# Self attention in four column tiles, and engine loops written out, in a small diffusion transformer

## The reference, cut to what matters

```python
h = (1 + scale_a) * layernorm(x) + shift_a
q, k, v = split(h @ W_qkv + b_qkv, 3)          # 16 heads of 8 features
o = softmax(q @ k.T / sqrt(8)) @ v             # self attention, 56 x 56 for each head
x = x + gate_a * (o @ W_proj + b_proj)
...
x = x + attention(layernorm(x) @ W_q, ctx @ W_kv) @ W_cproj   # 1500 context rows
x = x + gate_m * mlp((1 + scale_m) * layernorm(x) + shift_m)
```

## Time and profile before

| | us |
|---|---|
| median of 3 runs | 1056.95 (1056.18 to 1058.56) |
| the profiled execution | 1058.8 |
| its span, first to last instruction | 1057.0 |
| TensorE busy | 920.5 (87%) |
| VectorE busy | 575.2 (54%) |
| ScalarE busy | 509.2 (48%) |
| GpSimd busy | 362.3 (34%) |

### The profile page before, as it was taken

How to read it: one execution, slowest core, us unless ns; L and a number is a source line. 1 busy time by engine, 2 the same in 40 slices (tenths; PEclk the granted TensorE clock), 3 DMA queues, 4 the chain that set the end, 5 groups by cost and what they waited for, 6 DMA issues and landing times.

```text
span 1057.0 us, 24684 instructions
## 1 busy us (share of the span) xinstructions
PE 920.5 (87%) x9363; PEld 595.3 (56%) x9363; DVE 575.2 (54%) x1265; ACT 509.2 (48%) x754; POOL 362.3 (34%) x481
## 2 busy tenths in 40 slices
PE   5758999999787897978999999988698899999977
PEld 3435666666554444943666666654494466666653
DVE  7566566667232564135666666615313666666725
ACT  5555666665412114212666666531413366666541
POOL 6654555561000115046655554010312333333000
PEclk9688999999999996666999999999858799999999
DMA  9752443337327204316334333110413544443200
GB/s 261 174 146 60 118 119 103 106 88 244 120 75 205 59 0 124 84 39 160 102 105 111 106 110 88 27 59 1 126 43 95 132 118 118 117 116 88 61 1 9
DMA packets 76824, 106.27 MB, mean 101 GB/s; under 512 B 9370, under 2 KB 70426, under 8 KB 76480
## 3 DMA queue, kind: packets, MB, share of 16 engines
q1 hardware_dynamic: 75152, 102.26, 34.9%
q10 hardware_dynamic: 1584, 2.79, 0.9%
HBM read 41.17 MB, written 0.23 MB: 39 GB/s over the span
## 4 chain that ended last, share of the span: by engine, by line
PE 58%; DVE 15%; issue 14%; ACT 6%; POOL 3%; DMA 2%; SPq 1%; ACTq 0%; POOLq 0%; DVEq 0%
PE oacc_ps L579 10%; PE ring_ps L553 9%; PE score_ps L567 7%; PE ring_ps L537 6%; DVE max_sb L686 6%; PE ring_ps L530 6%; PE oacc_ps L895 4%; PE ring_ps L1173 3%; PE oacc_ps L334 2%; PE ring_ps L543 2%; PE ring_ps L522 2%; ACT key_sb L641 1%; POOL hat_sb L755 1%; DMA prob_sb<-ctx_T 1%; DMA nat_sb<-ctx_nat 1%
## 5 line engine op out<-in xcount | busy, mean ns | idle before, releaser
L686 DVE TENSOR_REDUCE max_sb<-ring_ps 128x1 f32<-128x500 f32 x576 | 356.3, 672 | 175.8 <-PE ring_ps L553 175.8
L659 ACT ACTIVATE prob_sb<-score_ps 125x896 f32<-125x896 f32 x288 | 257.2, 919 | 133.1 <-PE score_ps L567 132.2
L553 PE MATMUL ring_ps<-kstack,qstack 128*128 128x500 bf16 x576 | 204.4, 393 | 24.7 <-DVE max_sb L686 16.8
L764 POOL TENSOR_TENSOR key_sb<-key_sb,part_sb 128x500 f32<-128x500 f32 x72 | 81.9, 1137 | 282.8 <-ACT key_sb L641 282.8
L567 PEld LDWEIGHTS score_ps<-qstack,kstack 128*128 128x128 bf16 (+1 forms) x2304 | 145.4, 102 | 48.8 <-issue 8.1
L567 PE MATMUL score_ps<-qstack,kstack 128*128 128x112 bf16 (+3 forms) x2304 | 167.5, 214 | 2.5 <-ACT qstack L663 2.3
L579 PE MATMUL oacc_ps<-prob_sb,val_sb 125*32 125x168 f32 (+1 forms) x3456 | 140.2, 295 | 12.7 <-ACT prob_sb L659 12.3
L579 PEld LDWEIGHTS oacc_ps<-prob_sb,val_sb 125*32 125x32 f32 x3456 | 98.1, 110 | 51.9 <-ACT prob_sb L659 23.6
L553 PEld LDWEIGHTS ring_ps<-kstack,qstack 128*128 128x128 bf16 (+1 forms) x576 | 52.6, 98 | 111.1 <-issue 59.8
L755 POOL TENSOR_SCALAR hat_sb<-nat_sb,norm_now 125x128 f32<-125x128 f32 x192 | 87.6, 471 | 5.0 <-POOL norm_now L745 5.0
L771 POOL TENSOR_TENSOR part_sb<-key_sb,part_sb 128x500 bf16<-128x500 f32 x72 | 81.7, 1134 | 5.8
(11 more groups left out here) (208 smaller groups left out, 1038.0 us busy)
## 6 DMA issues: line engine op xcount, KB each, us to landing
kstack<-part_sb SPq DMA_DIRECT2D x432, 125.0 KB, 2.4
nat_sb<-ctx_nat SPq DMA_DIRECT2D x22, 672.0 KB
nat_sb<-ctx_T SPq DMA_DIRECT2D x8, 750.0 KB, 4.4
qstack<-qpart_sb SPq DMA_DIRECT2D x24, 224.0 KB, 3.6
w_sb<-ctx_nat SPq DMA_DIRECT2D x5, 672.0 KB
w_sb<-weights SPq DMA_DIRECT2D x1, 3076.5 KB, 12.7
prob_sb<-ctx_T SPq DMA_DIRECT2D x4, 750.0 KB, 7.3
tok<-ctx_nat SPq DMA_DIRECT2D x3, 672.0 KB
```

The costliest lines, as they stand in the source:

```text
L553: last = pe.matmul(ps[:, 0:KB], queries(p, n, D), kstack[:, u, p, j * KB:(j + 1) * KB], start=True, stop=True)
L659: ins = act.activation(dst, score_ps[0:CK, c % 2, :, 0:HALF], ACT.Exp)
L686: ins = dve.tensor_reduce(max_sb[:, p, j:j + 1], ring_ps[:, self.bank[name], 0:KB], AX.X, ALU.max)
L764: ins = pool.tensor_tensor(rest, rest, part_sb[:, 0, cols], ALU.subtract)
```

## The change

What it does:

- Self attention: the values are the weights now (56 x 32, of which the first 8 columns belong to the head), the probabilities move (56 columns). The four heads 4a to 4a+3 go to four column tiles, so a batch is 4 x 4 matmuls, and the result stands feature by token, with heads on partitions 0, 32, 64, 96 of four rows `a`. Four more matmuls with weights of ones and 4 x 56 moving columns give the sums. Two PSUM banks take turns. VectorE takes the reciprocal of 128 x 224 sums and multiplies 128 x 224 results, batch by batch; transposes and the bias step are gone.
- The bias of v is added by two matmuls in the stage that makes the values.
- The projection takes four products for each pair of batches, with weights that are spread over 4 x 128 rows with zeros between, and the first three pairs run in the stage.
- All engine loops are written out, and addresses and counts are constants. `settle` is removed wherever it stood.

```diff
-def later_periods(body, eng, after_first=None):
+def later_periods(body, after_first=None):
...
-    with eng.Fori(0, (B - 4) // 2) as j:
-        body((2 * j, 0, j), (2 * j + 1, 1, j), (2 * j + 2, 0, j + 1), (2 * j + 3, 1, j + 1))
-        body((2 * j + 1, 1, j), (2 * j + 2, 0, j + 1), (2 * j + 3, 1, j + 1), (2 * j + 4, 0, j + 2))
+    for n in range(B - 4):
+        body(*((k, k % 2, k // 2) for k in range(n, n + 4)))
...
-        own_val = sb("own_val", [LQ, B, NH, OW])
+        own_val = sb("own_val", [LQ, B * D + GW])
...
+        own_o = tok[:, 7:11, :]
...
-        def settle(eng):
-
-            eng.sem_inc(settled, 1)
...
+                self.banks = [oacc_ps[:, :], ring_ps[:, 1, :]]
+
+            def outputs(self, n, part):
+
+                cols = OWN_ROWS * LQ
+                return self.banks[n % 2][:, part * cols:(part + 1) * cols].rearrange("p (a q) -> p a q", q=LQ)
...
                 for b in range(B):
                     last = pe.matmul(score_ps[0:LQ, 0, b // 4, (b % 4) * D:(b % 4 + 1) * D], by_batch(xh_t)[:, b, :],
-                                     self.wval, start=True, stop=True)
+                                     self.wval, start=(b % 4 == 0), stop=False, skip_group_check=True)
+                for i in range(2):
+                    last = pe.matmul(score_ps[0:LQ, 0, i, :].rearrange("p (b k) -> p b k", b=4),
+                                     self.bval.broadcast_to([D, LQ]),
+                                     ident[:, :].unsqueeze(1).broadcast_to([D, 4, D]), start=False, stop=True,
+                                     skip_group_check=True)
...
-                def pair(i, more):
-                    pe.wait_ge(s["normed"], i + 1)
-                    for r in range(2):
-                        pe.wait_ge(s["probs"], 2 * i + r + 1)
-                        for h in range(NH):
-                            last = pe.matmul(oacc_ps[0:LQ, (r * NH + h) * OW:(r * NH + h + 1) * OW],
-                                             prob_sb[0:LQ, r, h * LQ:(h + 1) * LQ], own_val[:, 2 * i + r, h, :],
-                                             start=True, stop=True)
-                        last.then_inc(s["attended"], 1)
...
+                def attend(n):
+
+                    r = n % 2
+                    if n >= 2:
+                        pe.wait_ge(s["finished"], n - 1)
+                    pe.wait_ge(s["probs"], n + 1)
+                    probs = prob_sb[0:LQ, r, :].rearrange("p (a t q) -> p a t q", t=4, q=LQ)
+                    for a in range(OWN_ROWS):
+                        for t in range(4):
+                            at = n * D + (4 * a + t) * HD
+                            pe.matmul(self.outputs(n, 0)[t * GW:(t + 1) * GW, a, :], own_val[:, at:at + GW],
+                                      probs[:, a, t, :], start=True, stop=True, skip_group_check=True)
+                    for t in range(4):
+                        last = pe.matmul(self.outputs(n, 1)[t * GW:(t + 1) * GW, :, :], own_val[:, B * D:B * D + GW],
+                                         probs[:, :, t, :], start=True, stop=True, skip_group_check=True)
+                    last.then_inc(s["attended"], 1)
...
+                for n in range(B):
+                    attend(n)
+                    if n + 2 < B:
+                        scores(n + 2, n % 2)
+                    if n >= 3 and n % 2:
+                        pe.wait_ge(s["finished"], n - 1)
+                        project(pe, (n - 3) // 2)
+                pe.wait_ge(s["finished"], B)
+                project(pe, B // 2 - 1)
...
+                for n in range(B):
+                    act.wait_ge(s["scores"], n + 1)
+                    if n >= 2:
+                        act.wait_ge(s["attended"], n - 1)
+                    act.activation(prob_sb[0:LQ, n % 2, :].rearrange("p (h q) -> p h q", h=2),
+                                   score_ps[0:LQ, n % 2, :, 0:HALF], ACT.Exp).then_inc(s["probs"], 1)
...
+                sums = T(6)[:, 0:OWN_ROWS * LQ].rearrange("p (a q) -> p a q", q=LQ)
+                for n in range(B):
+                    dve.wait_ge(s["attended"], n + 1)
+                    if n:
+                        dve.wait_ge(s["finished"], n)
+                    dve.reciprocal(sums, self.outputs(n, 1)).then_inc(s["sums"], 1)
+                    dve.wait_ge(s["sums"], n + 1)
+                    dve.tensor_tensor(own_o[:, :, n * LQ:(n + 1) * LQ], self.outputs(n, 0), sums, ALU.mult)\
+                        .then_inc(s["finished"], 1)
...
+        def project(l):
+
+            def product(pe, i):
+                cols = slice(2 * i * LQ, 2 * (i + 1) * LQ)
+                for a in range(OWN_ROWS):
+                    last = pe.matmul(d_mid[l].ps("proj")[:, cols], w(NAMES[l]["proj"], a), own_o[:, a, cols],
+                                     start=(a == 0), stop=(a == OWN_ROWS - 1))
+                if i == B // 2 - 1:
+                    d_mid[l].pe.done(last, "proj")
+            return product
...
-                keep_busy(pe, 2)
-                pe.wait_ge(*last_output(att_own[l]))
-                d.product(pe, "proj", [(w(nm["proj"]), o_t)])
```

More of the change, by code:

```diff
@@ L33 @@
 FIRST_ROW = 2
-OW = HD + 1
+OWN_ROWS = 4
 GW = 32
@@ L796, in later @@
                 emit = self.emitter(eng)(engine)
-                later_periods(lambda *batches: self.run(eng, engine, emit, *batches), engine, after_first)
+                later_periods(lambda *batches: self.run(eng, engine, emit, *batches), after_first)
             def load_nat(self, sp, n, u):
@@ L833, in sync_later @@
                 self.sync_batch(sp, (0, 0, 0), (1, 1, 0))
-                with sp.Fori(0, (B - 4) // 2) as j:
-                    self.sync_batch(sp, (2 * j + 1, 1, j), (2 * j + 2, 0, j + 1))
-                    self.sync_batch(sp, (2 * j + 2, 0, j + 1), (2 * j + 3, 1, j + 1))
+                for n in range(1, B - 3):
+                    self.sync_batch(sp, (n, n % 2, n // 2), (n + 1, (n + 1) % 2, (n + 1) // 2))
                 self.sync_batch(sp, (B - 3, 1, B // 2 - 2), (B - 2, 0, B // 2 - 1))
@@ L914, in tensor @@
                     scores(r, r)
-                for i in range(B // 2):
-                    pair(i, i < B // 2 - 1)
+                for n in range(B):
[7 more added lines that the diff above has]
+                project(pe, B // 2 - 1)
             def scalar(self, act, meanwhile):
@@ L1823 @@
         a[name] = a[name][..., cols]
+    for name in ("L2_W_proj", "L3_sa_proj_w"):
+        rows = np.zeros((OWN_ROWS, 4, GW, D), np.float32)
+        rows[:, :, 0:HD, :] = a[name].reshape(OWN_ROWS, 4, HD, D)
+        a[name] = rows
     blocks = [a[name].reshape(n, D, cols).transpose(1, 0, 2).reshape(D, n * cols) for name, n, cols in WEIGHTS]
```

62 lines of the change are left out of this document (7 added, 55 removed), and 4 rows, old and new, of the table WEIGHTS.

## The result

The changed kernel takes 1018.05 us (median of 1014.28, 1017.0, 1019.09 and 1021.3), the kernel before 1056.97 beside it: a ratio of 0.9629, 95% interval 0.9592 to 0.9665. On a second chip it was 1016.9 us, 0.9637 (0.9619 to 0.9655). The forecast was 1013.5 us; the range of 1004 to 1030 holds it.

What follows compares the result with a forecast made beforehand. The prediction took TensorE to bound self attention, at a low clock; 1058.8 - 28 (self attention) - 14.5 (periods) - 1 (markers) = 1015.3 us, lowered by 1.85 us to a median of 1013.5 us, range 1004 to 1030.

Steps and rivals of the forecast that it cites:

- TensorE's batch: New self attention: attention 0.9 us, scores 0.48 and half a pair's projection 0.5, together 1.9 us at the high clock.
- Rival (1): Self attention: TensorE stays the bound at the high clock, 2.4 us a batch, 1019.5 us; chance 0.12.
- Rival (4): Self attention: column tiles don't run side by side, weight loads set each record, slower than before, 1075 us; chance 0.03.
- VectorE's batch: New self attention: reciprocal 1.55 us, multiply 0.38 and two gaps of 0.04, 2.01 us a batch, which becomes the bound.
- VectorE's share of the stretch: Self attention in the profile after: VectorE busy for about 97% of the 18 us stretch.
- The clock in the stage: New self attention: granted clock of 1.00, as TensorE's batches are as dense as the context attention.
- rival (2): Self attention: the clock falls in the stage as before, so it gains nothing, 1041 us; chance 0.08.
- the last projection: End of the self attention stage: 1.14 us, the time of line 1210.
- Self attention together: L2 and L3: stage gains of 13.0 and 13.1 us, plus 0.9 us behind each, 28 us.
- The bias products: Before the key work: two 512-column matmuls, 1.9 us, hidden in L2 by the GpSimd wait; up to 0.6 us in L3.
- The periods: Context attention loops written out: 12.7 us from looped batches and 1.8 from batch 0 in three layers, 14.5 us.
- the markers: Removing the settle increments, one before line 663: 0.05 us in some 20 batches, 1 us.

Runs made afterwards that it cites:

- short reciprocal: The changed kernel with self attention's reciprocal taken over only the first 56 of the 224 columns of sums: 1003.58 us, 0.9482.
- doubled reciprocal: The changed kernel with VectorE's reciprocal of self attention computed twice in each batch: 1042.53 us, 0.9848.
- settle_kept: The changed kernel with the increments on the semaphore settled put back behind each batch, all periods still written out: 1018.89 us, 0.9643.
- packed kernel: The changed kernel with the four heads of a column tile laid one under another on its partitions, leaving VectorE 56 columns instead of 224: 1016.44 us, 0.9621.

## Why the prediction was right, and where it was off

**TensorE's batch: right.** Forecast 1.9 us: 0.9, 0.48 and 0.5. The rows show 0.90 and 0.49, and the short reciprocal 1.41 us for the two and 0.47 for half a projection, 1.88 a batch. That it was not the bound rested on 0.1 us in my sum, and it held. Rival (1) fell with its two terms: the attention group takes 0.90 us with the switch to column tiles and back inside it, and the 32 small records take 12 to 13 ns each: their weight loads begin 0.37 us before those of the wider ones (416.78 to 417.15), their matmuls 0.42 us (416.78 to 417.20). By the Trainium skill (TensorEngine Tiling (Array Packing), Performance Considerations, Instruction Overhead) they would have cost 25 ns each, as an estimate from that page; the trace doesn't agree for records that alternate over four column tiles. Rival (4) wanted 95 ns a record at the low clock and fell with the same rows; its break-even comes, by its own 28.8 us a stage, to about 67 ns, not 75.

**VectorE's batch: the mechanism right, the size 0.08 us short.** The reciprocal was forecast at 1.55 us and is 1.56, the multiply 0.38 and 0.39. The gaps I took as twice 0.04: the one between them is 0.03 (422.00 + 1.56 to 423.59), but from a multiply to the next reciprocal it is 0.1 (421.50 + 0.39 to 422.00). 2.09 instead of 2.01 makes 0.6 us a layer. The doubled reciprocal shows that all of it is on the path. VectorE's share of the stretch was to be 97%; it is 15.58 of 17.60 us, 89%, as the wait for batch 0 is in it and the gaps are larger.

**The clock in the stage: right, but for its end.** It stayed at 0.99, against rival (2). Term mis-sized: the last projection, 2.05 us instead of 1.14. I had costed it at the high clock without asking what TensorE does meanwhile: it stands idle for 2.12 us while VectorE does the last batch. I had looked for the cause of a low clock only in the dense part.

**Self attention together:** 11.6 and 11.7 us in the stages and 0.9 and 0.7 behind them, 24.9 us where I had 28. The missing 3 us are twice 0.6 and 0.9 for the two terms above, and 0.2 behind L3's stage. The bias products are in their forecast place, 1.88 us long (order of time, changed kernel).

```profile
392.10 1.88 PE L840 MATMUL score_ps<-ident,vec_sb 128*56 128x512 f32 x4
...
395.23 0.65 PE L506 MATMUL ring_ps<-ident,hat_sb 125*128 125x125 f32 x4 [0.24 <-POOL hat_sb L732]
```

The transposes behind them still wait for GpSimd (0.24 us, 0.39 before), so the cover in L2 was real and thin. In L3, where I saw no such cover, the stretch from VectorE's read of the queries (line 1333, 1336 before) to the first attention matmul is 25.94 us (25.71 before): 0.2 us came out of the up to 0.6.

**The periods: right in place and size, the cause right as far as it went.** I had put the cost to addresses that are worked out in registers, without naming an engine; it is nearly all in TensorE's loop, and at the turn of the batch. Forecast 14.5 us and 1 for the markers. Alone on the chip both were 15.9 (0.9829 to 0.9859, so 14.9 to 18.1). In the profiles the four looped batches of the three layers win 13.5 us where I had 12.7, and the batch in front of them, from its first exponential to theirs, 2.6 us in the three layers where I had 1.8. The 1 us of the markers doesn't come out of the noise: settle_kept lies 0.8 to 2 us above the changed kernel with overlapping intervals, and its batches are 0.07 and 0.05 us longer in L0 and L2 and 0.05 shorter in L3. The code that the longer program has to fetch cost nothing in the periods, as forecast: 26.4 us a batch with 15 packets more. In the packed kernel it did cost.

**The sum and the median.** The sum against the profiled execution was 1015.3 us, and that execution took 1014.28. That they meet so closely is luck, as two errors cancel: 3 us too much for self attention and about 4 too little for the rest. Of the rest, 1.6 us are in the periods, and 1.4 in what goes before them in this execution, whose first exponential of line 640 stands at 72.21 us where line 659's stood at 73.62. The largest piece is one that I had not forecast at all: in L2 the stretch from VectorE's read of the queries of self attention to the first attention matmul, in which the first keys and values of the context are made too, took 27.04 us where it had taken 29.93. The clock was low in less of it: its mean was 0.87 against 0.71. The repeat of the changed kernel had 29.06 there, so this gain is not the change's in every run. Against it stand 1.2 us more between the context attention of L0 and that read, in a part that the change leaves as it was. Of the 1 us that I had taken for the marker increments the traces show at most a part. The forecast's median was 4.5 us too low, for another reason. I took off 1.85 us because the profiled execution of before lay above its median. The changed kernel's profiled execution was the fastest of its four, and these spread over 7 us (1014.28 to 1021.3) where the runs of before spread over 2.4; on the second chip it was 7.4 and 4.5. Their mean granted clocks were 0.944, 0.942, 0.936 and 0.934, in the order of their times, so the spread goes with the clock; each run kept only one trace, so what a slower execution of the same kernel loses can't be seen. But the stretch between the last exponential of L0 and the read of the queries in L2, which no experiment touches, takes from 110.6 to 114.7 us in the profiled executions of the 14 kernels, so some of the spread arises there.

## What to carry to other kernels

When one engine's part of a stage is cut, price the next engine's step, gaps between its instructions included, and look at what the first engine does while it waits: a pause at the end of the stage cost a low clock for the step behind it. Results laid out for the matrix engine's convenience (224 columns with 32 of 128 partitions in use) are paid for by the vector engine in columns, so pack them on the partitions, but count the instructions that this takes. Loops over registers are best judged engine by engine: here TensorE's cost most by far. When an engine pauses with no wait named, count its instructions from the end of one pause to that of the next, and look at the instruction queue's packets.

## What the hardware showed unexpectedly

- Small FP32 records in four column tiles follow each other at 12 to 13 ns (32 of 56 columns in 0.37 to 0.42 us); in the packed kernel 64 with their weight loads take 0.93 us (419.31 to 420.24), 14 to 15 ns each.
- TensorE can run out of instructions: at 146 a batch in 1.42 us it stopped for up to 1.81 us with no wait. The ends of these pauses lie 256 instructions apart, and 1.15 to 1.48 us behind the landing of a packet of 16384 bytes. At 116 a batch in 1.5 to 1.7 us it hardly stopped.
- A pause of 2.12 us was followed by a projection at 0.50 of the clock (2.05 us), one of 0.40 us by one at the high clock (1.15 us). In the packed kernel the clock was low behind the pause of 1.81 us (0.93 us for scores that take 0.57).
- A reciprocal costs VectorE 0.51 us for 56 columns, 0.86 for 112 and 1.56 for 224, at 128 partitions: 6.25 ns a column and 0.16 us.
